# Attention with its row maxima 24 steps ahead of the scores in place of 32, four units to a loop turn, and constant rows set by the pool

## What is computed

```python
def _dmha(x, Wr, Wqkv, Wp, bp):          # x: (batch, 4096 pixels, 288)
    xr = x @ Wr.T                        # 288 -> 144
    qkv = (xr @ Wqkv.T)                  # q, k, v; 8 heads of 18
    n = N // N_CHUNKS                    # 4 chunks of 1024 pixels
    attn = einsum('bhcnd,bhcmd->bhcnm', q, k) * scale
    attn = softmax(attn, axis=-1)
    o = einsum('bhcnm,bhcmd->bhcnd', attn, v)
    return o @ Wp.T + bp
t = t + _dmha(_ln2(t), Wr, Wqkv, Wp, bp)
t = t + _mlp(_ln2(t), W1, b1, W2, b2)
x = x + fold(t)                          # patches added back to pixels
```

## Time and profile before

| | us |
|---|---|
| median of three runs | 12761.37 (12758.24 to 12763.55) |
| profiled execution | 12757.43 |
| its span on the core | 12755.6 |
| TensorE busy | 12098.4 (95%) |
| VectorE busy | 8919.5 (70%) |
| ScalarE busy | 7556.9 (59%) |
| GpSimd busy | 3737.3 (29%) |
| row maxima on VectorE, 8192 | 5178.4 |
| exponentials on ScalarE, 8192 | 4393.7 |

### The profile page before, as it was taken

How to read it: one execution, slowest core, us unless ns; L and a number is a source line. 1 busy time by engine, 2 the same in 40 slices (tenths; PEclk the granted TensorE clock), 3 DMA queues, 4 the chain that set the end, 5 groups by cost and what they waited for, 6 DMA issues and landing times. The chain is left out here.

```text
span 12755.6 us, 252307 instructions
## 1 busy us (share of the span) xinstructions
PE 12098.4 (95%) x71228; PEld 4438.5 (35%) x71228; DVE 8919.5 (70%) x16555; ACT 7556.9 (59%) x15286; POOL 3737.3 (29%) x3524
## 2 busy tenths in 40 slices
PE   6999999999995699999999999999999999999899
PEld 2333333333332233333333333333333333333233
DVE  6777777777776577777777777777777777777211
ACT  4666666666664266666666666666666666666411
POOL 4767777777773000000000000000000000000243
PEclk9999999999997699999999999999999999999999
DMA  3101101101013333333333333333333333333355
GB/s 79 23 16 23 23 16 23 22 16 23 16 23 108 92 75 80 87 76 76 87 77 78 84 82 76 83 83 75 81 85 76 77 87 76 77 85 76 79 120 110
DMA packets 957932, 843.94 MB, mean 66 GB/s; under 512 B 658772, under 2 KB 693172, under 8 KB 945332
## 3 DMA queue, kind: packets, MB, share of 16 engines
q1 hardware_dynamic: 955060, 818.75, 28.5%
q10 hardware_dynamic: 1536, 8.39, 0.3%
HBM read 577.74 MB, written 247.05 MB: 65 GB/s over the span
## 5 line engine op out<-in xcount | busy, mean ns | idle before, releaser
L1580 DVE TENSOR_REDUCE a_big<-a_mp 128x1 f32<-128x512 f32 x8192 | 5178.4, 683 | 1917.4 <-PE a_mp L1417 1911.7
L1503 ACT ACTIVATE a_ex<-a_sc 128x512 f32<-128x512 f32 x8192 | 4393.7, 601 | 1723.7 <-PE a_sc L1405 1719.7
L1417 PE MATMUL a_mp<-a_ks,a_qs 108*128 108x512 bf16 x8192 | 3129.8, 383 | 47.2 <-DMA a_ks<-qk_parts 26.3
L1405 PE MATMUL a_sc<-a_qs,a_ks 111*128 111x512 bf16 x8192 | 3123.6, 383 | 40.5 <-issue 30.2
L546 POOL TENSOR_TENSOR r_prod<-r_temp,r_win 128x512 f32<-128x512 f32 x1792 | 2095.6, 1189 | 1158.6 <-ACT r_temp L845 939.1
L893 DVE TENSOR_TENSOR r_prod<-r_pg,r_win 128x512 f32<-128x512 f32 x2816 | 1846.5, 683 | 784.5 <-PE r_pg L618 444.2
L1431 PE MATMUL a_po<-a_ex,a_va 128*32 128x512 f32 x16384 | 2217.0, 606 | 12.2 <-issue 10.8
L1405 PEld LDWEIGHTS a_sc<-a_qs,a_ks 111*128 111x128 bf16 x8192 | 795.5, 97 | 2587.8 <-ACT a_ex L1503 1735.6
L1325 POOL TENSOR_TENSOR a_on<-a_oc,a_zb 128x512 f32<-128x512 f32 x256 | 325.1, 1270 | 3505.1 <-DMA a_zb<-z_rows 3505.1
L1313 POOL TENSOR_TENSOR a_pieces<-a_left,a_pieces 128x512 bf16<-128x512 f32 x256 | 295.6, 1155 | 3323.9 <-ACT a_pieces L1489 3323.9
L1417 PEld LDWEIGHTS a_mp<-a_ks,a_qs 108*128 108x128 bf16 x8192 | 801.7, 98 | 983.1 <-DVE a_big L1580 300.5
(11 more groups left out here) (180 smaller groups left out, 11113.9 us busy)
## 6 DMA issues: line engine op xcount, KB each, us to landing
a_qs<-qk_parts SPq DMA_DIRECT2D x768, 144.0 KB
a_ks<-qk_parts SPq DMA_DIRECT2D x768, 144.0 KB
qk_parts<-a_pieces SPq DMA_DIRECT2D x128, 768.0 KB, 5.0
f_t<-mixed SPq DMA_DIRECT2D x48, 1536.0 KB, 16.4
a_tw<-second SPq DMA_DIRECT2D x512, 128.0 KB, 3.0
a_zb<-z_rows SPq DMA_DIRECT2D x256, 256.0 KB
mixed<-a_t SPq DMA_DIRECT2D x256, 256.0 KB, 5.5
r_win<-first SPq DMA_DIRECT2D x128, 280.5 KB, 5.0
```

Source lines behind the costliest of these rows:

```text
L1405: pe.matmul(sc[k % BANKS][:, :], ks[0:KROWS + NPART, p.h, head, 128 * kb:128 * kb + 128], qs[0:KROWS + NPART, p.h, head, CHUNK * qb:CHUNK ...
L1417: pe.matmul(mp[k % BANKS][:, :], qs[0:KROWS, p.h, head, 128 * q:128 * q + 128], ks[0:KROWS, p.h, head, CHUNK * half:CHUNK * half + CHUNK], ...
L1503: nc.scalar.activation(ex[:, k % RING, :], sc[k % BANKS][:, :], ACT.Exp, scale=scale).then_inc(exped.sem, 1)
L1580: nc.vector.tensor_reduce(big[:, x % 2, k // 2:k // 2 + 1], mp[k % BANKS][:, :], AX_X, ALU.max).then_inc(maxed.sem, 1)
```

## The change

1. **`LEAD = 24`.** A new function `leading(p, t, which)` tells the step whose maxima stand in step t: step t + 24 of the same unit while t < 8, else step t - 8 of the next. So the negation of a unit's second quad is at the end of its own t = 7, that of the next unit's first quad at t = 23. `TASKS` moves the transpositions from 0 and 18 to 9 and 25, three pieces that stood from 9 to 12 one step back, and v's third piece from 25 to 22. In unit -1 there are maxima from t = 8 only; unit 63 has some for t < 8.
2. **SP.** `load_max(p, 1)` goes from the head of the unit to behind `gather_sums(p, 0)`; `gather_sums(p, 2)` goes ahead of `load_max(p + 1, 0)`.
3. **The loop's body is four units**, 15 turns for the same 60 units.
4. **Constants.** The pool sets the ones of `ks` and raises `rows_set`, for which SP waits before the first `load_stack`. ScalarE waits for `prepared` only before its first v piece.

```diff
-TASKS = {0: (0, "max", 1), 1: (-1, "out", 0), 2: (-1, "out", 1), 4: (2, "qk", 0), 5: (2, "qk", 1), 7: (2, "qk", 2),
+TASKS = {1: (-1, "out", 0), 2: (-1, "out", 1), 4: (2, "qk", 0), 5: (2, "qk", 1), 7: (2, "qk", 2),
...
+LEAD = 24
...
-        with engine.bass.Fori(0, units // 2 - 2, engines=bass.OrderedEngineSet([engine.engine]), hint_back_edge=True) as i:
-            unit(Pass(2 * i + 2, 0, i + 1), (-1, 0, 1, 2))
-            unit(Pass(2 * i + 3, 1, i + 1), (-1, 0, 1, 2))
+        assert units % 4 == 0
+        with engine.bass.Fori(0, units // 4 - 1, engines=bass.OrderedEngineSet([engine.engine]), hint_back_edge=True) as i:
+            for k in range(4):
+                unit(Pass(4 * i + k + 2, k % 2, 2 * i + k // 2 + 1), (-1, 0, 1, 2))
...
+def leading(p, t, which):
+
+    u = t + LEAD
+    if u < STEPS:
+        return (p, u) if 0 in which else None
+    return (p.to(1), u - STEPS) if 1 in which else None
...
             if 0 in which:
-                load_max(p, 1)
                 if -1 in which:
...
                 gather_sums(p, 0)
+                load_max(p, 1)
                 spread_inverses(p, 0)
...
                     sp.wait_ge(prepared, 1)
+                    sp.wait_ge(rows_set, 1)
                 load_stack(a, 0)
             if 0 in which:
                 spread_inverses(p, 1)
+            if 0 in which:
+                gather_sums(p, 2)
             if 1 in which:
                 load_max(p.to(1), 0)
             if 0 in which:
-                gather_sums(p, 2)
                 spread_inverses(p, 2)
...
+        nc.gpsimd.memset(ks[96:128, :, :, :], 1.0).then_inc(rows_set, 1)
+        pool.wait_ge(rows_set, 1)
...
-                    if 1 in which:
-                        maximum(p.to(1), t, x)
+                    if leading(p, t, which):
+                        maximum(*leading(p, t, which), x)
...
-        act.wait_ge(prepared, 1)
...
+                if k == 0 and isinstance(own.n, int) and own.n == 0:
+                    act.wait_ge(prepared, 1)
                 act.wait_ge(v_made.sem, v_made.at(own.n, k + 1))
...
-        nc.vector.memset(ks[96:128, :, :, :], 1.0)
...
-                if 1 in which and t % 16 == 15:
-                    negate(p.to(1), t // 16)
+                if leading(p, t, which) and (t + LEAD) % 16 == 15:
+                    own, u = leading(p, t, which)
+                    negate(own, u // 16)
```

More of the change, by code:

```diff
@@ L1013, in bank_before @@
     return max(j for j in range(PER_UNIT - BANKS, PER_UNIT) if j % BANKS == k % BANKS) - PER_UNIT + 1
-TASKS = {0: (0, "max", 1), 1: (-1, "out", 0), 2: (-1, "out", 1), 4: (2, "qk", 0), 5: (2, "qk", 1), 7: (2, "qk", 2),
-         8: (-1, "out", 2), 9: (2, "qk", 3), 10: (-1, "out", 3), 11: (2, "qk", 4), 12: (-1, "out", 4),
-         15: (1, "v", 0), 18: (1, "max", 0), 20: (1, "v", 1), 25: (1, "v", 2)}
+TASKS = {1: (-1, "out", 0), 2: (-1, "out", 1), 4: (2, "qk", 0), 5: (2, "qk", 1), 7: (2, "qk", 2),
+         8: (-1, "out", 2), 9: (0, "max", 1), 10: (2, "qk", 3), 11: (-1, "out", 3), 12: (2, "qk", 4), 13: (-1, "out", 4),
+         15: (1, "v", 0), 20: (1, "v", 1), 22: (1, "v", 2), 25: (1, "max", 0)}
+LEAD = 24
 INVERT = {2: (-1, 3), 10: (0, 0), 18: (0, 1), 26: (0, 2)}
@@ L1106, in attention_phase @@
     prepared = sem("prepared")
+    rows_set = sem("rows_set")
     zw_in = [Signal(sem(f"zw_in{h}"), 48) for h in range(2)]
```

## The result

The changed kernel takes 12735.28 us (median of 14 executions, 12722.5 to 12747.02), the kernel before 12761.93 on the same chip (12752.51 to 12774.47). The ratio is 0.9978, with a 95% interval of 0.9971 to 0.9986: 27 us faster, where 45.5 were forecast. The time lies in the range, and the sum is off by 19 us. The terms are further off than the sum: two large ones, of which the prediction knew one, nearly cancel.

A forecast was written before the change was run, and what follows sets the result against it. In steady state TensorE was taken as full, so reordering wins only in its gaps. Terms -37.2 - 8.6 - 4.0 + 4.3 + 4 - 4 = -45.5 us took the median 12761.4 to 12716 us; range 12690 to 12748.

The forecast's parts named there:

- Four units in a turn: Loop's back edges: 14 in place of 29, 15 fewer at 2.48 us each, -37.2 us, bounds 20 to 50 less.
- edges cost by code: Rival 1, loop's back edges: cost grows with body length, so 14 cost what 29 did; 12753 us, chance 0.08.
- Where the steady unit changes: Loop's units: negation and transposition move to other steps, near net zero, +0.06 x 60 = +4 us, bounds -20 and +27.
- the same 0.3 comes back there: Step t = 23 of each unit: nothing hides the negation there, so about 0.3 us saved at the unit's head returns.
- Rival 2: Negation at t = 23 is dear, VectorE behind for two steps: +0.45 us a unit, 12739 us, chance 0.10.
- Constant rows by the pool: Start of the attention phase: ScalarE's first cast no longer waits for VectorE's memsets, -8.6 us, bound -2.5.
- the 36 of the estimate: Pool's memset of ks: 36 us by the Trainium skill's 2.6 GpSimd cycles per element, making the sum some 4 us worse.
- everything to the end of the phase hangs on it: Start of the attention phase: the first cast coming 8.6 us earlier moves all that follows.
- Lead of 24, ahead of unit 0: Before unit 0: 32 maxima leave the stretch VectorE paces, so unit 0 starts earlier, -4.0 us, bounds -9 and +2.
- Lead of 24, at the end: Unit 63: 32 maxima in its first 8 steps make it TensorE-paced there, +4.3 us.
- SP's queue: Unit 62: zc lands some 4 us earlier with SP's new order, though the stall largely stays; -4 us, bounds -8 and 0.
- Rival 3: zc(0) too late in every unit, VectorE standing for it, each us costing 61: 12808 us, chance 0.06.

The follow-up runs named there:

- after_two: The changed kernel with the loop body back at two units a turn (29 back edges): 12710.7 us, ratio 0.9967 to the kernel before.
- before_rows_by_pool: The kernel before with only the change's constants edits (pool sets ones of ks, ScalarE's first casts don't wait): 12748.65 us, ratio 0.9998.
- best_rows_by_vector: The change with v's third piece at 23 and two units a turn, constant rows set by VectorE again, ScalarE waiting: 12661.55 us, ratio 0.9922.
- best_sp_order_back: The change with v's third piece at 23 and two units a turn, SP's two swaps undone: 12666.02 us, ratio 0.9929.
- before_end_moved: The kernel before with 380 do-nothing waits (191 instructions) ahead of TensorE's attention code, moving the loop's branch from place 8 to 199: 12710.29 us, ratio 0.9963.

## Why the prediction was right in its range and wrong in its terms

- **"Four units in a turn", -37.2.** Measured -44.0 (one execution of each), and the place in the trace was right: TensorE's empty queue behind the branch. The step that failed is the price. I divided 72.0 by 29 and took 2.48 us for a property of an edge. It is one of the place of the branch: 0.0 to 2.6 us for the same branch. The term came near by luck, because the change puts the branch at 5, nearly as bad as the 8 of before. Alone on the kernel before, where it puts the branch at 72, the same edit gives 60 us. The rival "edges cost by code" was wrong too. Its argument, that dear and cheap edges differ threefold and no row says why, was the loose end to pull. That the Trainium skill ("Advanced Engine Details and Errata", Control Flow Timing) gives 108 ns for the branch agrees with the edges of `after_two`, which show nothing over it.
- **"Where the steady unit changes", +4.** Measured +44 in one execution and +33 in the other, beyond the bound of +27. The gain that I counted was right: steps 0 and 1 got 0.33 us shorter, and 0.06 of it went into step 9. (It was four pieces, not three, that moved one step back, those of steps 9 to 12.) The step that failed is "the same 0.3 comes back there". Uncovered, the negation costs 1.0 us a unit. My row for it was the old place, where an output projection follows one step later and takes the rest. Rival 2 named the mechanism and gave it 0.45 a unit. The 1.3 us of VectorE's absence and then seven banks at 0.61 against TensorE's 0.44 carry further than the 0.66 us by which one step is overfull (4 x 0.60 + 1.1 - 2.84). Two of the prediction's own signs said so in the first profile: unit 1 took 117.90 us where 117.3 within 0.3 was forecast, and steps 24 and 25 together 6.75, over 6.5.
- **"Constant rows by the pool", -8.6.** The first cast moved by 8.5 as forecast. The pool's memset is done in time, and the row that was missing is here:

```profile
4199.21 13.75 POOL L1345 MEMSET a_ks<- 32x16384 bf16 x1 [224.01 <-POOLq L1940]
```

  13.75 us, VectorE's time and the lower bound, and not the 36 of the estimate. The step that doesn't hold is "everything to the end of the phase hangs on it": it took the clock of one execution for given. Unit 0 came 7.7 us earlier in `before_rows_by_pool`, but no later in `best_rows_by_vector`.
- **"Lead of 24, ahead of unit 0", -4.0.** With an early cast unit 0 starts 153.8 and 155.4 us after the first projection in the old order, and 145.9 to 149.6 in the new (mean 148.4), so -6 from mean to mean: right in sign, within the bounds.
- **"Lead of 24, at the end", +4.3.** Measured +4.3.
- **"SP's queue", -4.** Unit 62 gained 1.8 us in the profiled pair. Over all profiles it took 112.0 to 117.5 us with the change's SP order and 116.8 to 120.2 with the old one, 3.5 us more on the mean, so sign and size are about right. The stall is 6.20 us for zc where it was 8.70; it lay in the forecast 5 to 9:

```profile
11753.70 0.60 SPq L1248 DMA_DIRECT2D a_zc<-a_oc  x1
...
11755.60 0.25 DVE L1590 RECIPROCAL a_zr<-a_zc 128x16 f32<-128x16 f32 x1 [6.20 <-DMA a_zc<-a_oc]
```

- **Rival 3, zc late in every unit.** It did not come: VectorE waited 8.2 us for it in the whole loop. Its price was wrong as well: in `best_sp_order_back` 59 us more of lateness cost 13, about 0.2 a us, not 1.

## What to carry to other kernels

Small serial work on an engine that reads TensorE's banks belongs directly ahead of a piece of TensorE work that needs none of those banks; here moving a piece of 1.5 us by one step was worth 0.4% of the kernel. Before a loop is unrolled because its edges cost, count the instruction fetches of the page against the number of edges and look at where the branch lies: code that moves for other reasons can make edges dear or free, and so can hide the effect of an edit, or look like one. A price found by dividing a total by a count is a mean of unlike things until the spread is explained.

## What the runs showed of the hardware

- TensorE runs through a loop's end without a gap, or stalls up to 2.6 us on the mean, by where the branch lies among pieces of 256 instructions. Places 253, 5 and 8 cost 1.5 to 2.6 us an edge. At 199 the step behind the edge was as long as any other (3.05 us) in the five kernels with a lead of 24. In the old order 0.5 us an edge were left at 199 and 0.8 at 72, where VectorE's own edge, 0.6 us behind an uncovered negation, has a part. The Trainium skill ("Runtime: NRT & Kernel Launch", Instruction fetch mechanics) says that code comes in blocks of 16 KiB and that a taken branch to a block that isn't at hand waits for its fetch. The size agrees (11.70 MB in 714). That the same branch is free at one place and costs most just behind a border is what these runs add. The exact border is open.
- TensorE's clock rose to 2.4 GHz after it had stood idle for over 9 us between two projections, in two of three executions (0.74 and 0.75 over the five projections), and stayed near 1.2 GHz (0.50 to 0.55) in eleven where they came 1.4 us apart. By the issue of the next window, less waiting cost nearly as much as it saved.
- An instruction that holds two waits already met costs TensorE an estimated 0.11 us of its stream (191 of them fill the stretch from 4207.98 to 4228.93 in `before_end_moved`).
- The pool sets 16384 elements per partition (32 partitions) in 13.75 us, VectorE in 13.71.
